# Down products of four more units in three f32r passes: one edit of a decoder layer on Trainium2

## The reference

```python
topk_idx, tw = _route(x, router_w, bias)
combine = (jax.nn.one_hot(topk_idx, E, dtype=tw.dtype) * tw[..., None]).sum(1)
h = jnp.einsum('td,edf->etf', x, gate_w)
u = jnp.einsum('td,edf->etf', x, up_w)
y = jnp.einsum('etf,efd->etd', jax.nn.silu(h) * u, down_w)
routed = jnp.einsum('etd,te->td', y, combine)
sh = jax.nn.silu(x @ sh_gate_w) * (x @ sh_up_w) @ sh_down_w
return (routed + sh).reshape(hidden_states.shape)
```

## Time and profile before

| | |
|---|---|
| median of 3 runs | 193.97 us (193.88 to 194.04) |
| the profiled execution | 193.8 us |
| its span, first to last instruction | 192.1 us |
| PE busy | 176.5 us, 92% |
| DVE busy | 141.4 us, 74% |
| POOL busy | 120.1 us, 63% |
| ACT busy | 107.6 us, 56% |

### The profile page before, as it was taken

How to read it: one execution, slowest core, us unless ns; L and a number is a source line. 1 busy time by engine, 2 the same in 40 slices (tenths; PEclk the granted TensorE clock), 3 DMA queues, 4 the chain that set the end, 5 groups by cost and what they waited for, 6 DMA issues and landing times.

```text
span 192.1 us, 4580 instructions
## 1 busy us (share of the span) xinstructions
PE 176.5 (92%) x1685; PEld 132.8 (69%) x1685; DVE 141.4 (74%) x309; ACT 107.6 (56%) x211; POOL 120.1 (63%) x177
## 2 busy tenths in 40 slices
PE   5899989999799889999987989999999999999992
PEld 5678776667665547677776856666668888888882
DVE  5784485878886896989898869994456776776565
ACT  6458687666774554444585465352346556655550
POOL 4484699855675626665654313017999999998800
PEclk9999999999999999999999999999999999999999
DMA  5986400001113000000000000617993654400003
GB/s 149 306 236 174 123 3 5 2 3 31 31 44 110 3 0 0 0 0 3 2 0 0 3 0 9 249 31 216 367 291 92 212 157 157 137 21 0 0 2 109
DMA packets 17718, 15.75 MB, mean 82 GB/s; under 512 B 2224, under 2 KB 13568, under 8 KB 17568
## 3 DMA queue, kind: packets, MB, share of 16 engines
q1 hardware_dynamic: 16832, 15.13, 25.6%
q10 hardware_dynamic: 864, 0.33, 0.6%
HBM read 14.86 MB, written 0.59 MB: 80 GB/s over the span
## 4 chain that ended last, share of the span: by engine, by line
PE 64%; DVE 13%; ACT 8%; POOL 8%; issue 6%; DVEq 0%; POOLq 0%
PE banks L1488 5%; PE banks L1527 4%; PE banks L1509 4%; PE banks L1514 4%; PE banks L1512 4%; PE banks L1510 4%; PE banks L1513 4%; PE banks L1511 4%; PE banks L1316 3%; POOL kbd L487 3%; PE banks L1531 3%; PE banks L1532 3%; PE banks L1530 3%; DVE sum L1027 3%; DVE mx L1017 2%
## 5 line engine op out<-in xcount | busy, mean ns | idle before, releaser
L770 ACT ACTIVATE s<-banks 128x512 f32<-128x512 f32 x36 | 21.3, 598 | 29.9 <-PE banks L1511 29.6
L495 POOL TENSOR_TENSOR act<-act,vbd 128x512 f32<-128x512 f32 x14 | 22.2, 1587 | 2.6 <-DMA vbd<-comb_rows 1.4
L646 POOL TENSOR_TENSOR gu_lo<-gu_w,gu_hi 128x256 fp32r<-128x256 f32 x14 | 11.3, 810 | 16.1 <-ACT gu_hi L776 16.1
L487 POOL TENSOR_TENSOR kbd<-kbd,rs 128x1024 f32<-128x1024 f32 x7 | 13.3, 1902 | 12.6 <-DVE rs L1031 12.6
L1151 DVE TENSOR_TENSOR act<-s,banks 128x512 f32<-128x512 f32 x20 | 13.6, 685 | 10.1 <-ACT s L770 7.5
L495 POOL TENSOR_TENSOR qk_fold<-qk_fold,vbd 128x512 f32<-128x512 f32 x12 | 19.1, 1600 | 0.8 <-DVE qk_fold L1151 0.4
L1151 DVE TENSOR_TENSOR qk_fold<-s,banks 128x512 f32<-128x512 f32 x16 | 10.9, 687 | 9.2 <-PE banks L1514 5.8
L1509 PE MATMUL banks<-x3hi,gu_lo 128*128 128x512 f32 x36 | 16.7, 465 | 0.3 <-DVE qk_fold L1151 0.3
L764 ACT COPY p2T<-banks 128x512 f32<-128x512 f32 x16 | 8.6, 588 | 14.3 <-PE banks L1476 14.2
L1488 PE MATMUL banks<-vo_fold,p2T 128*128 128x128 f32 x128 | 16.0, 278 | 0.5 <-ACT p2T L764 0.5
L1488 PEld LDWEIGHTS banks<-vo_fold,p2T 128*128 128x128 f32 x128 | 14.9, 191 | 1.3 <-ACT p2T L764 1.1
(11 more groups left out here) (178 smaller groups left out, 466.3 us busy)
## 6 DMA issues: line engine op xcount, KB each, us to landing
vbd<-comb_rows SPq DMA_DIRECT2D x30, 256.0 KB, 3.7
wkv_sb<-in_L_xattn_w_kv_dram SPq DMA_DIRECT2D x1, 1024.0 KB, 8.2
gu_w<-in_L_ffn_gate_w_dram SPq DMA_DIRECT2D x16, 64.0 KB, 2.7
gu_w<-in_L_ffn_up_w_dram SPq DMA_DIRECT2D x16, 64.0 KB, 3.0
vo_fold<-in_L_ffn_down_w_dram SPq DMA_DIRECT2D x1, 960.0 KB, 5.6
wq_sb<-in_L_xattn_w_q_dram SPq DMA_DIRECT2D x1, 512.0 KB, 5.9
wout_sb<-in_L_xattn_w_out_dram SPq DMA_DIRECT2D x1, 512.0 KB, 6.5
x<-in_x_dram SPq DMA_DIRECT2D x3, 128.0 KB, 3.0
```

The costliest lines, as they stand in the source:

```text
L487: engine.tensor_tensor(p2[:, t % 4, :, :], p2[:, t % 4, :, :], rs2[:, t % 2, :].unsqueeze(2).to_broadcast([P, H2, CTX]), ALU.mult).then_in ...
L495: engine.tensor_tensor(act_of(k), act_of(k), spread[:, j % SPREAD, :], ALU.mult).then_inc(scale_early if j < RING else scale_s, 1)
L770: sc.activation(sil[:, k % 2, :], bank[2 * (k % 2)], ACT.Silu).then_inc(sil_s, 1)
```

## The change

Units 8 to 11 leave the list `WHOLE` and so become parted: their down products are made of three f32r passes from rounded and rest activations. ACT gets four more rounds and DVE four more rests, written into the hand-made order. The code on PE and POOL is not edited. The three pairs of buffers are dealt out by position among the parted units, so unit 12 now takes the second pair where it took the first.

```diff
-        WHOLE = [0, 1, 3, 4, 2, 5, 6, 7, 8, 9, 10, 11]
+        WHOLE = [0, 1, 3, 4, 2, 5, 6, 7]
...
             silu(13)
+            round_act(8)
             silu(14)
+            round_act(9)
+            round_act(10)
+            silu(15)
+            round_weights(10)
+            round_act(11)
             round_act(12)
-            for k in range(15, NK - 1):
+            round_act(13)
+            for k in range(16, NK - 1):
                 silu(k)
...
             multiply(13)
+            rest_act(8)
             multiply(14)
+            rest_act(9)
+            rest_act(10)
+            multiply(15)
+            rest_act(11)
             rest_act(12)
-            for k in range(15, NK - 1):
+            rest_act(13)
+            for k in range(16, NK - 1):
                 multiply(k)
                 rest_act(k - 2)
```

## The result

The changed kernel takes 204.64 us in the median of five executions (202.06 to 205.56), the kernel before beside it on the same chip 193.88 (193.75 to 194.04). The ratio is 1.050, with an interval of 1.043 to 1.057; it leaves out the two longest executions (205.16 and 205.56), which lie over 1.5% above the fastest, so it is smaller than the ratio of the two medians. Slower was right, and the waits that were forecast are there, but the time lies above my 201.7 and outside the range of 199.0 to 202.6.

What follows compares the result with a forecast made beforehand. The prediction took the number and price of PE passes, plus holes in PE's queue, as the bound. Holes of 8.3 us with the 0.64 saving inside gave 7.7 us later: 193.8 + 7.7 = 201.5, median 201.7, range 199.0 to 202.6.

Steps and rivals of the forecast that it cites:

- What bounds the kernel, and the saving: Expert stage: PE's passes set the time, without holes; four down products become 0.16 us cheaper each, 0.64 in all.
- Where the waits come: PE waits for DVE's rests ahead of downs 8, 9, 11, between 136 and 151 us, 7 to 8 us in all.
- Hole 1: Ahead of down 8: rest 8, behind multiply 13 and POOL's weight rest, ends at 138.01; gate_up 14 comes 2.07 us late.
- the mark: Second pass of a gate_up on PE (L1510), used to follow lateness: forecast 2.07, 4.86, 7.7 us late for units 14, 15, 16.
- The whole sum: Three holes of PE between units 13 and 16, 8.3 us, make gate_up 16 7.7 us late with the 0.64 saving inside.
- Rests beside POOL, and the slip-in: DVE's rests wait their turn with POOL's operations, ending 0.55 us behind them; a waiting POOL operation goes between two rests.
- (a): Rival on DVE's rest pairs: POOL slips in never or only once, giving 199.7 or 200.7 us; chance 0.30.
- Restarts: PE after a wait: a gate_up's second pass comes 1.14 us behind the rest's end, 1.84 with a second down between.
- (e): Rival on PE's restarts: weights loaded ahead across the wait save up to 0.19 us each over five, 200.8 us; chance 0.04.
- Carried whole: Behind unit 16 PE stays full to the end, so the 7.7 us of lateness is not paid back.
- (c): Rival on units 12 to 30: POOL paces them, the delay is paid back and 0.64 stays, 193.3 us; chance 0.03.
- (d): Rival: PE's clock falls to 1.2 GHz from gate_up 14 to down 12, up to 6.3 us more, 207.9; chance 0.06.

Runs made afterwards that it cites:

- the last pair of runs: Most of POOL's scaling of units 10 to 17 cut, in the changed kernel with downs one gate_up later (193.38 us) and in the kernel before (193.68 us).
- half the fill: Changed kernel with half as many unread PE transposes (6, 6, 2, 5, 2) ahead of downs 8 to 12: 202.92 us.
- the fill: Changed kernel with unread PE transposes (12, 12, 4, 10, 4) ahead of downs 8 to 12, while PE waits: 201.59 us.
- one hole of 1.94 us: Against the changed kernel, only unit 8 parted: with rest 12 behind multiply 15, 196.77 us; with rest 12 in its old place, 197.13 us.
- the control: The kernel before with POOL scaling only 8 of 512 columns of units 10 to 17: 193.68 us, ratio 1.001.

## Why the prediction missed, point by point

- **What bounds the kernel, and the saving.** Right. PE's passes set the time, and the saving of 0.64 is borne out by the last pair of runs (0.30 gained, 0.36 lost in a gap).
- **Where the waits come.** Right: the holes are ahead of downs 8, 9 (and 10), 11 (and 12), all between 136 and 152 us, and ahead of unit 13 on there is none. PEld's waits are 8.7 in five, where 7 to 8 in three or five was written.
- **Hole 1.** Right: the mark was forecast 2.07 late and is 2.14 late, and rest 8 ends at 136.74 + 1.28 = 138.02, for 138.01.
- **The whole sum.** The 7.7 holds at full clock: 7.58 with half the fill, mark by mark, and 7.73 with the fill, there in part by luck.
- **Rests beside POOL, and the slip-in.** Right in kind. Both pairs had a scaling in between, 2.37 each, where I had 2.74 (from 141.17 to 143.91) for the first; POOL was done with its queue at 141.64, and at the slow clock rest 9 came only at 142.16. The second scaling began within rest 11 and ended at 151.31, ahead of down 12 (151.91), so it was rest 12 that stood behind it, as forecast. So (a) falls.
- **Restarts.** (e) falls: the wait of the weight load goes along with that of its matmul, as in the earlier trace rows, and the marks of the half-filled kernel leave no 0.19 a restart over.
- **Carried whole.** Right, so (c) falls. From 160 to 190 us PE is busy 30.00 of 30.00, and the lateness of the end is that of the last slow pass.
- **The step that failed: (d), the clock.** I gave it 0.06 because the clock stayed at 1.00 while PE was busy 8.47 of 10 us with waits up to 1.3, and the range left it out. The changed kernel repeats that row unchanged (8.46, 1.00). But it is no test of what came next: in 136 to 140 us PE was busy 1.96 of 4 us, with one hole of 2.04, and the clock fell; in 140 to 144, at half clock, it was 2.56. A row with shorter holes and much more work in between can't bound it. Rows with such holes did not exist in the trace, and I should have read that as unknown from both sides, with (d)'s upper end in the range, instead of as evidence against. That end was itself miscounted: from gate_up 14 to down 12 are 24 passes, 27 only with down 8, so 5.6 and 207.3 instead of 6.3 and 207.9; and the slow passes did not stop there, eight more came behind mark 16.
- **What the clock took,** by the marks of the profiled run. From mark 14 to multiply 14 are 141.55 - 139.12 = 2.43 where 1.41 was worked out: 1.02. From the end of rest 10 (142.16 + 2.37 = 144.53) to mark 15 are 1.92 for 1.14: 0.78. The rest pair was 0.37 shorter. With hole 1's 0.07 these give 1.02 + 0.78 - 0.37 + 0.07 = 1.50, and 6.36 - 4.86 is 1.50. From mark 15 to mark 16 are 6.65 (153.10 - 146.45) where I had 5.77 (150.82 - 145.05): 0.88 more. Here multiply 15 too stands 2.43 behind its mark, 1.02 more than worked out, but 0.24 come back, since rest 11 did not meet POOL's weight rest (over at 149.25): it ended at 150.17, 3.72 behind the mark, for 2.94. The other 0.10 lie behind rest 11, where the clock falls again. Behind mark 16 eight passes at half clock take 156.37 - 153.10 = 3.27, at full clock 8 x 0.233 = 1.86: 1.41. Together 7.68 + 1.50 + 0.88 + 1.41 = 11.47, less the 0.10 by which this trace was ahead 11.37: the 11.3 of the spans. So 3.8 us lie beyond my 7.7: the clock took some 4.3, and 0.6 were given back by rests that met less of POOL.

The Trainium skill, TensorE: Matmul & The Clock Gate, section HAM oscillation — how this bites in real kernels, describes a kernel whose waits for DMA between bursts of work throw the clock back each time. Its waits are longer than those here. The trace agrees in part: the clock falls at 139.1, behind the first wait, is back at 149.5 to 150.0, within the third, and falls again at 152.7, behind the fourth. With one hole of 1.94 us it fell in one profiled run and not in the other. I had the section before me and weighed it less than a row that did not bear on it.

Which of the executions lose how much stays open. With the holes filled it is nothing (but for the fall at 60 to 70 us), with half the fill nothing in the one execution that was profiled, without fill 0.5 to 4.0, taking 201.59 as the time without a fall.

## What to carry to other kernels

Before work is moved onto a longer chain (round, rest, then product), look at what stands directly in front of the product in PE's queue. A product right behind the matmuls that its own input comes from makes PE wait for the whole chain, and saving 0.16 four times was paid with 7.6 us of waits and restarts at full clock.

Holes in a PE that was full before can cost more than their length. Put the clock into the range unless the trace holds a row with holes as long and work between them as little; if the hole can't be avoided, idle matmuls in it are cheap insurance (here they gave back 3 of 11 us, and half as many held the clock in the run that was profiled).

Moving the product later only helps as far as the engine that feeds it has room. Here DVE's rests and POOL's work take turns, so the room was that of both together.

## What the runs showed of the hardware

- The clock falls, and comes back, within a few microseconds and not the same way each time. Two kernels with the same hole of 1.94 us gave, in the profiled runs, one a fall at once and one none. And a fall between 60 and 70 us, far ahead of any edit, costs 1.2 us; two profiled runs show it (the filled kernel and the one with unit 8 alone and rest 12 in place). One run of ten of the control (194.87, clock 0.989) and single runs of the kernel before (194.84, clock 0.989) have about the same loss and clock, but were not profiled. Why there, I can't say.
- At the half level a pass starts 0.43 behind the last and is 0.63 long, for 0.23 and 0.40 at the full one.
- DVE's multiply, which has one input in PSUM, takes 0.67 to 0.69 beside a POOL that never stops (137.84 and 141.25 above), the rest of the same size, with both inputs in SBUF, 1.18. The Trainium skill, SBUF — State Buffer, section Who interferes with whom, says that a DVE instruction with two SBUF inputs contends with POOL instructions that read SBUF, and that one with at most one SBUF input, outside its two-port modes, doesn't. The traces agree: 0.68 against 1.18. A waiting POOL operation gets its turn between two DVE operations in a row: pairs of rests take 2.37 and 2.88 with a scaling waiting, 1.28 where the scaling was held back, and 1.29 where it was left out.
- Transposes of 128x128 that PE does ahead of a wait keep its clock up: 1.00 from 136 to 156 us with 12, 12, 4, 10 and 4 of them and with half as many, where the changed kernel has 0.50 for 8 us.
